# Metaformer layer with spectral attention on one core: the token mix takes its stationary operands from a ring of contiguous columns that GpSimd fills

## The reference, cut to what matters

```
x = x + conv(_ln_c(x))                      # _ln_c: layer norm over the last axis

def codano_forward(x, ...):                 # conv
    tokens_norm = instance_norm(tokens)
    k, q, v = fno_layer(tokens_norm, ...)   # spectral convolution plus a 1x1 skip
    dprod = softmax(q . k / scale)          # over the 32 tokens of a batch entry, 16 heads
    attn = fno_layer(dprod @ v, proj...)
    attn = instance_norm(attn + tokens, attn_norm_g, attn_norm_b)
    m = instance_norm(attn, norm2_g, norm2_b)
    m = fno_layer(m, mixer 1, norm, gelu)
    m = fno_layer(m, mixer 2, norm)
    return instance_norm(m) + attn

t = x as (4, 4096*4, 128) tokens;  Wx = batch_norm(_ln_t(t) @ W.T)
t = t + ys,  ys[i] = sigmoid(Wx[i] + ys[i-1] @ V.T)   # a recurrence, solved by guess and check
```

## Time and profile before

| what | value |
|---|---|
| median of 3 runs | 619.43 us (617.39 to 620.93) |
| profiled execution | 622.1 us, span 620.3 us from first to last instruction |
| PE busy | 444.6 us, 72% of the span |
| DVE busy | 423.5 us, 68% |
| POOL busy | 259.6 us, 42% |
| ACT busy | 241.7 us, 39% |
| mean granted TensorE clock | 0.843 of full speed |

### The profile page before, as it was taken

How to read it: one execution, slowest core, us unless ns; L and a number is a source line. 1 busy time by engine, 2 the same in 40 slices (tenths; PEclk the granted TensorE clock), 3 DMA queues, 4 the chain that set the end, 5 groups by cost and what they waited for, 6 DMA issues and landing times.

```text
span 620.3 us, 7899 instructions
## 1 busy us (share of the span) xinstructions
PE 444.6 (72%) x2517; PEld 356.2 (57%) x2517; DVE 423.5 (68%) x1065; ACT 241.7 (39%) x485; POOL 259.6 (42%) x264
## 2 busy tenths in 40 slices
PE   0687999999734467999889940846655654989591
PEld 0677999996500117999878940834332321656391
DVE  5899366731889886012499969477888755788792
ACT  1465310101110103332455501236888896768300
POOL 0534810000567710000898793667557609910000
PEclk9999965555956877999989975868999998889796
DMA  8820000032500001000004551000000000000099
GB/s 352 272 57 2 1 5 0 1 89 48 131 6 0 0 2 51 1 0 1 1 2 119 171 156 48 2 1 0 2 0 2 1 0 1 1 0 0 2 274 269
DMA packets 40341, 32.04 MB, mean 52 GB/s; under 512 B 4640, under 2 KB 37840, under 8 KB 39280
## 3 DMA queue, kind: packets, MB, share of 16 engines
q1 hardware_dynamic: 40304, 31.57, 17.2%
HBM read 21.01 MB, written 8.45 MB: 47 GB/s over the span
## 4 chain that ended last, share of the span: by engine, by line
PE 46%; DVE 36%; POOL 5%; ACT 5%; issue 4%; DMA 1%; DVEq 0%; SPq 0%; ACTq 0%
PE PS L588 43%; DVE SML L1035 6%; DVE BIG L1151 4%; PE PS L592 4%; POOL BIG L574 3%; DVE BIG L1332 3%; DVE BIG L1170 2%; POOL BIG L569 2%; DVE BIG L1412 2%; DVE SML L1346 2%; DVE BIG L364 1%; ACT BIG L894 1%; DVE BIG L1249 1%; DVE BIG L1245 1%; DVE BIG L1341 1%
## 5 line engine op out<-in xcount | busy, mean ns | idle before, releaser
L588 PE MATMUL PS<-CST,BIG 128*128 128x65 f32 (+6 forms) x1026 | 159.6, 359 | 8.5 <-DVE BIG L1332 3.3
L588 PEld LDWEIGHTS PS<-CST,BIG 128*128 128x128 f32 (+1 forms) x1026 | 146.1, 232 | 25.5 <-issue 13.7
L592 PE MATMUL PS<-CST,BIG 128*128 128x128 f32 (+2 forms) x460 | 76.6, 309 | 103.7 <-ACT SML L364 28.1
L592 PEld LDWEIGHTS PS<-CST,BIG 128*128 128x128 f32 (+2 forms) x460 | 62.0, 182 | 129.6 <-issue 79.1
L588 PE MATMUL PS<-BIG 128*128 128x128 f32 (+2 forms) x466 | 68.3, 458 | 27.9 <-DVE BIG L1151 14.6
L364 DVE COPY BIG<-PS 128x512 f32<-128x512 f32 (+2 forms) x49 | 32.7, 675 | 71.3 <-PE PS L592 38.4
L588 PEld LDWEIGHTS PS<-BIG 128*128 128x128 f32 (+2 forms) x466 | 45.2, 181 | 46.1 <-issue 16.9
L364 ACT ACTIVATE BIG<-PS 128x512 f32<-128x512 f32 (+5 forms) x53 | 29.9, 564 | 104.8 <-PE PS L588 71.0
L553 POOL TENSOR_TENSOR BIG<-BIG,SML 128x512 f32<-128x512 f32 x32 | 32.0, 1037 | 77.2 <-ACT BIG L931 77.2
L1035 DVE BATCH_NORM_STATS2 SML<-BIG 128x6 f32<-128x128 f32 x256 | 53.4, 277 | 7.4 <-DMA BIG<-in_x 6.3
L588 PE MATMUL PS<-SML,BIG 128*128 128x128 f32 x256 | 57.7, 387 | 0.5 <-DVE SML L1204 0.5
(11 more groups left out here) (210 smaller groups left out, 592.9 us busy)
## 6 DMA issues: line engine op xcount, KB each, us to landing
BIG<-in_x SPq DMA_DIRECT2D x8, 1024.0 KB, 12.1
BIG<-in_x SPq DMA_DIRECT2D x32, 256.0 KB, 2.9
out_x<-BIG SPq DMA_DIRECT2D x32, 256.0 KB, 3.6
BIG<-wy_rows SPq DMA_DIRECT2D x16, 128.0 KB, 3.5
BIG<-SML SPq DMA_DIRECT2D x16, 128.0 KB, 2.4
BIG<-in_L_conv_mixer_w SPq DMA_DIRECT2D x2, 544.0 KB, 6.3
CST<-in_const SPq DMA_DIRECT2D x1, 644.0 KB, 20.9
BIG<-in_L_conv_proj_w SPq DMA_DIRECT2D x1, 68.0 KB, 6.3
```

Source lines behind the costliest of these rows:

```text
L588: return pe.matmul(o, l, rhs, start=start, stop=stop, **k)
L592: return pe.matmul(o, i, ident[0:n, 0:n], is_transpose=True, start=True, stop=True)
```

## The change: what it does

GpSimd gets 32 new `tensor_copy` instructions between its last product and its wait for the mix. Copy g takes the four columns of group g out of `x_t` and lays each down contiguously in one of five places of a ring, `x_mix`. The ring is in `BIG3` from number 5632 to 8192, which the attention's copy of the modes (`xrep`, read by all products) had before and `ta1` has after; so the first copy waits until all 32 of VectorE's products and all 20 of GpSimd's are done. From the sixth copy on each waits until TensorE has finished the group that used its place. TensorE waits before each group for its copy and takes its stationary operands from the ring. The products are the same numbers in the same order; the ACT and DVE streams are as before.

```diff
+MIX_RING = 5
+PROD_DVE, PROD_POOL = 32, 20
...
+        x_mix = BIG3[:, 5632:5632 + 512 * MIX_RING].rearrange("t (k w h) -> t k w h", k=MIX_RING, h=H)
...
+            pool.wait_ge(S("prod_dve"), PROD_DVE)
+            pool.wait_ge(S("prod_pool"), PROD_POOL)
+            for g in range(32):
+                if g >= MIX_RING:
+                    pool.wait_ge(S("mix_filled"), g + 1 - MIX_RING)
+                pool.tensor_copy(x_mix[:, g % MIX_RING], x_t[:, :, 4 * g:4 * g + 4].rearrange("t h w -> t w h")
+                                 ).then_inc(S("x_mix"), 1)
             pool.wait_ge(S("kap"), 1)
             pool.wait_ge(S("a0"), 32)
             pool.wait_ge(S("mix_filled"), 32)
...
             for g in range(32):
                 if g >= 4:
                     pe.wait_ge(S("a0"), g - 3)
-                for w in range(4 * g, 4 * g + 4):
-                    last = mm(PS[:, 4 + g % 4, 128 * (w % 4):128 * (w % 4) + 128], x_t[:, :, w], acft)
+                pe.wait_ge(S("x_mix"), g + 1)
+                for w in range(4):
+                    last = mm(PS[:, 4 + g % 4, 128 * w:128 * w + 128], x_mix[:, g % MIX_RING, w, :], acft)
                 last.then_inc(S("mix_filled"), 1)
```

## The result

The changed kernel takes 599.75 us (median, 597.66 to 600.79) where the kernel before, in the same comparison, takes 619.66: a ratio of 0.968, 95% interval 0.965 to 0.971. That is 19.9 us less; 14 were forecast. The profiled execution has 599.96 us and a span of 598.2. The two profiled spans differ by more than the medians, 22.1 us, because the execution profiled before was 2.5 us above its median and the one after 0.2.

What follows compares the result with a forecast made beforehand. TensorE alone, through strided weight loads, was taken to bound the mix; copies at 1.3 us plus 7.5 us lost to VectorE would gain 14 us: 622.1 - 14 = 608 profiled, 2.7 lower at the median, 605.5, range 596 to 615.

Steps and rivals of the forecast that it cites:

- TensorE alone sets the mix, and the stride of its weight load sets TensorE: Token mix: only TensorE sets its end; contiguous columns cut a group from 1.76 to 0.89 us at full clock.
- the four spacings: Weight-load spacings behind the stride claim: mix 0.221 and P1 0.218 us strided, Gram 0.121 at most and X1 0.118 contiguous.
- Nor is the clock: Claim that clock does not explain slow loads: the mix at 1.00 is spaced as P1 at 0.57.
- The price of a copy, 1.3: GpSimd's strided copy of 128 x 512 numbers in the mix: 1.3 us each, setting the pace after the sixth copy.
- the forecast case: Main case, 60%: a copy takes 1.15 to 1.56 us, loss to VectorE 3 to 8 us, gains 5 to 23.
- cheap copies: Rival, 17%: mix copies take near 1.0 us or VectorE is not in the way; at 1.04, gain 21, time 598.
- the slow rival: Rival, 12%: a mix copy costs 2.08 us like the strided tensor_scalar; group 31 ends 6.7 us later, 626.
- POOL loses 7.5 us to VectorE: In the mix, GpSimd's copies lose 7.5 us to VectorE's operations, as waiting copies and operations can alternate throughout.
- What lies behind the last copy, 1.2 us: End of the mix: after the last copy at 281.0, hand-over 0.1 and group 0.89, so group 31 ends near 282.2.
- the bound (271.3): End of group 31 with TensorE alone and free copies: 271.3 against 296.39, at most 25.1 us to gain.
- The rival's condition: Clock rival, 8%: TensorE waits a third of each period, the clock falls and the mix ends 2 us later.
- The 32 added waits: TensorE's waits for copies in the mix: cost nothing while the copy is what is waited for.

Runs made afterwards that it cites:

- e1: The change with all copies and waits kept, but TensorE reading the image's strided columns as before: 620.26 us, 1.002 of the kernel before.
- e2: The change without copies and their waits, TensorE taking contiguous rows of the image instead of columns (other data): 594.99 us, 0.962 of the kernel before.
- e7: The change plus a five-place ring of GpSimd copies for P1's stationary operands, from token 16 on: 597.89 us, 0.967 of the kernel before.
- e3: The change with each copy reading four contiguous rows instead of four strided columns (other data): 594.52 us, 0.961 of the kernel before.
- e11: The change plus a P1 ring, 122 moving columns in P1, and mix copies eight ahead with waits for predecessors: 583.55 us, 0.943 of the kernel before.

## Why the prediction was right, point by point

*TensorE alone sets the mix, and the stride of its weight load sets TensorE*: right, and shown by e1 and e2 (0.220 a record with the strided operand, whatever else is changed; 0.113 without). But one of the four spacings that the argument rested on was misread. P1's 0.218 is no evidence for the stride: at its clock a contiguous load is spaced 0.213 (e7). "Nor is the clock" was true of the mix and not of P1, whose clock of 0.57 stood in the earlier trace rows; the pair Gram and mix, both at full clock, carried the argument alone. The warning stood in the earlier trace rows: the Gram group of 1.71 us is contiguous and spaced 1.71 / 8 = 0.214, P1's figure. The prediction put that down to the clock and did not carry it over to P1. (In the trace before, the clock reads 1.00 there, from 24 to 32; in the trace after, the same group of 1.71 us lies in a stretch, 25.5 to 29, that has 0.57.)

*The price of a copy, 1.3*: too high, 1.03, and outside the forecast case, which had T from 1.15 to 1.56. What came true is the rival "cheap copies", at 17%, in its size (T = 1.04) and its time (598); the stated range held it because it took in half of that case. The estimate of 1.24 beside it was too high as well. Linear scaling of the 16 x 128 copy was an upper bound; its fixed part is larger than the 0.08 that I took: (1.04 - 0.39) / 384 gives 1.7 ns a number, which leaves 0.17 (an estimate from two rows that differ in partitions too). The strided tensor_scalar, from which the slow rival came, is no guide to a copy.

*POOL loses 7.5 us to VectorE*: it lost 33.47 - 27 x 1.03 = 5.7. The size was near, the picture was wrong. They did not alternate during the first four products: those ran at full speed, and the copy stood still for 3 us; later ones took 1.5 to 2.0 us beside VectorE's operations. So zw came at 243.8 and not at 250.6, and ScalarE did not wait for it. The operations on single numbers, which I had not counted, then took a copy's length each, some 6 us in all, with slack to spare: z3_1 was complete at 260.1 (264 forecast), and TensorE did not wait for it.

*What lies behind the last copy, 1.2 us*: 3.5. At T = 1.03 the last eight groups are TensorE's own, 1.33 each with their transposes; this was in the bound (271.3) but not in the sum.

The sum of these for the end of group 31, forecast at 282.2: the ring opened 0.7 earlier with the mix, 27 x 0.27 = 7.3 less for the copies, 1.8 less for VectorE, 2.3 more behind the last copy, together 7.5 less, 274.7; it ended at 274.62. In the time, 605.5 against 599.75, part of this does not appear: the forecast took 2.7 us off for the distance between the profiled execution and the median, which was 0.2 after the change.

*The clock*: full from about 241, as forecast. The rival's condition, a TensorE that waits a third of each period, did not come about: at 0.89 of 1.03 us it waits a seventh. So what a third would do is not shown. *The 32 added waits*: nothing, as e1 shows.

## What to carry to other kernels

Look at the spacing of weight loads, not at TensorE's busy share: a load of 128 float32 columns was spaced 0.11 us only when its numbers were contiguous and the clock was at its upper level, and 0.21 to 0.22 when either was missing, so an engine with nothing to do may repack the operand, but only where the clock is up (and where it is not, widening the moving operand into unused columns may help: P1 with 122 columns instead of 65 ran at 1.00 instead of 0.50 and was 0.5 us longer by itself). Compare only stretches at the same clock before blaming a stride. When GpSimd streams copies beside VectorE, let each wait for its predecessor before giving it a longer lead: a deeper buffer without that made this kernel 6 us slower than the change, and with it no faster.

## What the runs showed of the hardware that was not expected

- GpSimd's copies, sent off far enough ahead that no wait held them, shut out a VectorE operation with two SBUF inputs until the last copy was done, 13.18 us for 128x1 numbers; a wait of each copy for its predecessor, which costs 0.1 us a copy, brought this to 1.01. Why the change itself, whose copies also follow on each other, gave way after every copy was not settled; its lead is five instead of ten.
- The shut-out has the other sign too: four two-input VectorE products in a row held one copy for 3 us. The Trainium skill, "SBUF — State Buffer" (Who interferes with whom), says that such an operation contends with a GpSimd read and that the one that comes second is blocked until the first is finished; the trace agrees for one pair (1.46 instead of 0.69), but here the one that waited was passed over by several operations in a row. In e3 and e11 a copy at the same place was let in after one product (0.61 and 2.06 us); what decides between the two is not shown.
- A strided GpSimd copy of 128 x 512 takes 1.04 us and a contiguous one 0.61, a factor of 1.7.
- A contiguous weight load at the 1.2 GHz level is spaced 0.21 us, as a strided one is at 2.4 GHz.
